# One excursion of ScalarE per block instead of two, and the first convolution on VectorE

## The reference

```
h1 = xg @ W1.T + b1 ; h2 = h1 @ W2.T + b2          # per group g of 512 tokens
xz = x @ Wi.T + bi                                   # 256 -> 1024
x_in, z = xz[..., :512], xz[..., 512:]
u  = silu(causal_depthwise_conv4(x_in) + conv_b)
dt = softplus(x_in[..., :32] @ Wdt.T + bdt)
A  = -exp(A_log)                                     # 512 x 16
h  = h * exp(dt_t * A) + dt_t * Bm * u_t             # per token, 512 x 16 states
y  = einsum('bdn,dn->bd', h, Cm)
out = (y * silu(z)) @ Wo.T + bo + x * mean(Dv)
```

## Time and profile before

| | us |
|---|---|
| median of 3 runs | 744.03 (739.25 to 746.37) |
| the profiled execution | 739.71 |
| its span, first to last instruction | 737.9 |
| VectorE busy | 648.1 |
| PE busy | 630.7 |
| ScalarE busy | 612.5 |
| GpSimd busy | 329.6 |

### The profile page before, as it was taken

One profiled execution on the slowest core, in us unless ns is written; L12 is line 12 of the kernel. 1 busy time (PEld: TensorE's weight loads), 2 busy tenths in 40 slices (PEclk: granted clock), 3 DMA queues, 4 the chain that ended last, 5 costly groups with the idle time before them and its releaser, 6 DMA issues.

```text
span 737.9 us, 8249 instructions
## 1 busy us (share of the span) xinstructions
PE 630.7 (85%) x2904; PEld 324.4 (44%) x2904; DVE 648.1 (88%) x443; ACT 612.5 (83%) x1077; POOL 329.6 (45%) x184
## 2 busy tenths in 40 slices
PE   7877986889886999999888999995894999698946
PEld 5632432264432365645344466542240473345524
DVE  2427855979999999999999999899999999999994
ACT  2487998689988998999798989999798888894771
POOL 0106202426799046897930638436992051080010
PEclk9997998899999899999898999999896999899979
DMA  8440747180738143160749170160608150705001
GB/s 286 169 171 16 233 138 228 58 256 9 280 116 298 69 151 105 38 235 24 275 144 301 42 256 2 52 234 29 228 15 271 50 207 24 261 15 214 30 0 58
DMA packets 40027, 103.08 MB, mean 140 GB/s; under 512 B 4081, under 2 KB 13041, under 8 KB 39985
## 3 DMA queue, kind: packets, MB, share of 16 engines
q1 hardware_dynamic: 37424, 94.40, 36.0%
q10 hardware_dynamic: 2560, 8.14, 4.9%
HBM read 23.08 MB, written 4.19 MB: 37 GB/s over the span
## 4 chain that ended last, share of the span: by engine, by line
PE 41%; ACT 33%; DVE 13%; DMA 6%; issue 5%; ACTq 1%; POOL 1%; SPq 0%; POOLq 0%; DVEq 0%
ACT G L1159 14%; DVE G L1328 11%; PE Y L1498 9%; PE MB L1526 6%; PE MB L1369 5%; PE MB L1443 4%; PE MB L1465 4%; ACT XN L976 3%; PE MB L1424 3%; ACT XI L1076 3%; PE MB L1476 2%; ACT L1129 2%; PE MB L1433 2%; DMA RV<-DW 2%; DMA W<-in_w 2%
## 5 line engine op out<-in xcount | busy, mean ns | idle before, releaser
L1328 DVE TENSOR_TENSOR_SCAN G<-G,RV 128x1024 f32<-128x1024 f32 (+3 forms) x256 | 535.7, 2153 | 33.9 <-ACT G L1159 19.3
L1159 ACT ACTIVATE G<-RD,COL 128x1024 f32<-128x1024 f32 (+1 forms) x288 | 279.5, 1043 | 19.2 <-PE Y L1498 16.7
L1498 PE MATMUL Y<-G,RW 128*32 128x512 f32 x1024 | 139.4, 660 | 39.5 <-DVE G L1328 39.5
L881 POOL TENSOR_SCALAR LV<-LV 128x4 f32<-128x4 f32 x18 | 19.7, 1097 | 227.2 <-ACT XN L976 227.0
L890 POOL TENSOR_TENSOR LV<-LV,HALF 128x4 f32<-128x4 f32 (+1 forms) x25 | 45.4, 1816 | 113.6 <-DVE LV L1222 112.1
L921 POOL TENSOR_SCALAR X<-X,LV 128x256 f32<-128x256 f32 x32 | 85.3, 2674 | 0.8
L1498 PEld LDWEIGHTS Y<-G,RW 128*32 128x32 f32 x1024 | 27.1, 114 | 117.0 <-DVE G L1328 61.0
L907 POOL TENSOR_SCALAR XN<-X,LV 128x256 f32<-128x256 f32 x36 | 76.8, 2137 | 1.9
L1465 PE MATMUL MB<-XI,DIAG 128*64 128x512 f32 x248 | 65.5, 666 | 13.9 <-DMA XI<-XI 13.9
L1526 PE MATMUL MB<-WO,ZS 128*128 128x256 f32 x256 | 62.7, 379 | 0.9 <-DVE ZS L1337 0.9
L1443 PE MATMUL MB<-XT,WI 128*128 128x512 f32 x128 | 62.5, 615 | 1.0 <-ACT XT L1002 1.0
(11 more groups left out here) (95 smaller groups left out, 777.1 us busy)
## 6 DMA issues: line engine op xcount, KB each, us to landing
RD<-DW SPq DMA_DIRECT2D x60, 512.0 KB, 3.8
RV<-DW SPq DMA_DIRECT2D x60, 512.0 KB, 5.3
W<-in_w SPq DMA_DIRECT2D x48, 256.5 KB, 4.0
XI<-XI ACTq DMA_DIRECT2D x30, 256.5 KB, 5.8
X<-in_x SPq DMA_DIRECT2D x8, 512.0 KB, 6.0
out<-X SPq DMA_DIRECT2D x7, 512.0 KB, 3.0
G<-in_w SPq DMA_DIRECT2D x4, 513.0 KB, 8.1
RV<-in_w SPq DMA_DIRECT2D x4, 513.0 KB, 12.9
```

The source lines that it names most:

```text
L1159: eng.activation(G[:, i % NG, 1 + t0:1 + t1], RD[:, q, t0:t1], ACT.Exp, scale=NAC[:, states(i):states(i) + 1]).then_inc(sems["exp"])
L1328: eng.tensor_tensor_scan(g[:, at:1 + t1], g[:, at:1 + t1], v[:, at:1 + t1], first, ALU.mult, ALU.add).then_inc(sems["scan"])
L1498: ins = eng.matmul(Y[32 * q:32 * q + 32, 512 * h:512 * h + 512], RW[:, states(i + o), :], G[:, (i + o) % NG, 512 * h + 1:512 * h + 513], s ...
```

## The change

It does nine things. (1) `dts` is dissolved: dm, the softplus load, dt, the silu load, u, the z of up to two blocks and the exp load stand in one stretch at the end of `proj`; "unset" is gone, so blocks 1 to 15 have three loads each and not four. (2) The convolution of the first half of block 0 is made by VectorE (`conv`: one multiplication by a tap, three multiply-adds over 512 tokens), out of an unsplit copy XC that ScalarE makes; the matrices DIAG0 and eight matmuls go. (3) Layernorms 0 to 3 and 23 take mean and variance by bn_stats and bn_aggr on VectorE, not by sums and squares. (4) All others centre with the mean: GpSimd's two instructions after 1/sqrt (L895, L900) become one before it (`mean`). (5) The shift DMAs of ten blocks (`SYNCED`) are issued by SP's queue. (6) VectorE takes over xi of block 1, the sums of layernorms 7 and 12, and the copies of layernorm 7's transposes. (7) The merge weights of the second group are loaded into ZS, not RV. (8) The order up to the first scans is given by a string, HEAD. (9) All tables of places are new.

```diff
-RATE, STORE = 220, 80
-FIRST = ["dts", "proj", "outs"]
+RATE, STORE = 300, 200
+FIRST = ["proj", "outs"]
...
-DTS, PROJ = (-21, -22, -25, -20), (-25, -25, -32, -27)
+PROJ = (-23, -26, -27, -26)
+MEET, LULL = 0, 3
...
-SENDS, LATE = (8, 9, 15, 15), (14, 14, 14, 15)
-REPD, REPL = 9, 11
+SENDS, LATE = (11, 11, 11, 15), (11, 12, 14, 12)
+REPD, REPL = 9, 9
...
+HEAD = "sscbcsccllbabllbalsbblsalbllllsl"
...
-VSUM, VXI, VXT = (), (), ()
+VSUM, VXI, VXT = (7, 12), ((1, 0), (1, 1)), (7,)
+SYNCED = (2, 3, 4, 6, 7, 8, 9, 10, 11, 12)
...
-    def dts(k):
...
-        yield from after(("w", k - 1, passes(k - 1) - 1))
-        yield 2
-        for hf in range(2):
-            do("dm", k, hf)
-        yield 0
-        do("softset", k, 0)
-        do("dt", k, 0)
-        do("unset", k, 0)
-
-    def proj(k):
...
+        if zs and zs[0] >= NZ:
+            yield from after(("opm", (zs[-1] - NZ) // 4, 1, 3))
+        for _ in range(MEET):
+            yield 0
+        yield from after(("repd", k - 1, 3, passes(k - 1) - 1), ("w", k - 1, passes(k - 1) - 1))
+        yield 2
+        for hf in range(2):
+            do("dm", k, hf)
         yield 0
+        do("softset", k, 0)
+        do("dt", k, 0)
         do("silu", k, 0)
         for hf in range(2):
             do("u", k, hf)
-        for ko in zs[:1]:
-            for hf in range(2):
-                do("z", ko, hf)
-        for ko in zs[1:]:
+        for ko in zs:
             for hf in range(2):
                 do("zm", ko, hf)
             for hf in range(2):
                 do("z", ko, hf)
         do("expset", k, 0)
-        yield from rest_for(REST)
-        yield from after(("dt", k, 0))
+        yield from rest_for(LULL)
         do("w", k, 0)
...
+                elif stage == "bn":
...
+                    for i in range(2):
-                        ins = eng.scalar_tensor_tensor(out=v[:, t, :], in0=bank("opa", *a)[:, 256 * i:256 * i + 256], scalar=1.0,
-                                                       in1=v[:, t, :], op0=ALU.mult, op1=ALU.add, accum_out=lv[:, 0, t:t + 1])
-                    ins.then_inc(sems["vop"])
+                        t = 2 * pr + i
+                        src = bank("fm", 0, 0, hf, pr)[:, 256 * i:256 * i + 256] if ph == 1 else v[:, t, :]
+                        ins = eng.bn_stats(out=gauge(c)[:, t, 0:6], in_=src)
+                    ins.then_inc(sems["bn"])
...
+                elif stage == "conv":
+                    e.wait_ge("xc", 0, 0)
+                    e.wait_ge("col")
+                    eng.tensor_scalar(CV, XC[:, 0:512], COL[:, CW0:CW0 + 1], None, ALU.mult).then_inc(sems["taps"])
+                    for t in range(1, 4):
+                        eng.wait_ge(sems["taps"], t)
+                        ins = eng.scalar_tensor_tensor(out=CV, in0=XC[:, t:t + 512], scalar=COL[:, CW0 + t:CW0 + t + 1], in1=CV,
+                                                       op0=ALU.mult, op1=ALU.add)
```

More of the change, by code:

```diff
@@ L114, in summed, with gauged @@
 def summed(c):
-    return "vsum" if early(c) or c in VSUM else "sum"
+    return "vsum" if c in VSUM else "sum"
+def gauged(c):
+    return c < 4 or c == 23
 def evac(k, hf):
-    return "vxi" if (k, hf) in VXI else "xi"
+    return "xc" if (k, hf) == (0, 0) else "vxi" if (k, hf) in VXI else "xi"
 def turned(c):
@@ L507, in begin @@
     def begin(k, s):
-        for first, chain in ((DTS, dts), (PROJ, proj)):
-            for ko in range(2, 16):
-                if 16 * k + s == 16 * ko + first[ko % 4]:
-                    yield chain(ko)
-        if (k, s) in PLAN["dts1"]:
-            yield dts(1)
+        for ko in range(2, 16):
+            if 16 * k + s == 16 * ko + PROJ[ko % 4]:
+                yield proj(ko)
         if (k, s) in PLAN["proj1"]:
@@ L541, in begin, with leads @@
             yield outs(3, 1)
+    def leads():
+        for i in range(LEAD):
+            do("exp", i)
+            yield 0
     def run(steps):
@@ L570, in schedule @@
     run(a)
+    do("diag")
     next(first)
     run(first)
-    for _ in range(3):
-        next(b)
+    do("rw")
     run(ffn(0, 0, 0))
-    for stage in ("diag", "rw"):
-        do(stage)
-    next(c)
-    for _ in range(5):
-        next(second)
-    next(c)
-    run(c)
-    a = half(0, 0)
-    for _ in range(4):
-        next(a)
-    next(second)
-    run(a)
-    run(b)
-    run(second)
-    next(late)
-    next(late)
-    for i in range(LEAD):
-        do("exp", i)
-    next(late)
-    next(late)
+    chains = {"a": half(0, 0), "b": b, "c": c, "s": second, "l": late, "e": leads()}
+    for name in HEAD:
+        next(chains[name], None)
+    for name in "cae":
+        run(chains[name])
+    for chain in (b, second):
+        needs[chain] = 0
     needs[late] = 0
@@ L956, in do @@
                     e.wait_ge(made("off", c), c)
-                    for i in range(4 if early(c) else 2):
+                    for i in range(4):
                         ins = eng.activation(xn[:, i, :], v[:, i, :], ACT.Identity, bias=lv[:, 4, i:i + 1],
@@ L1061, in do @@
                     if k:
-                        for hf in range(2):
+                        for hf in range(1 if k == 1 else 0, 2):
                             e.wait_ge("um", k - 1, hf)
@@ L1078, in do @@
                     ins.then_inc(sems["xi"])
-                elif stage == "sh":
+                elif stage == "sh" and a[0] not in SYNCED:
                     k, = a
-                    e.wait_ge("halo", k)
-                    e.wait_ge(evac(k, 1), k, 1)
+                    e.wait_ge(*(("halo", k) if k else ("xie",)))
+                    for hf in range(0 if k else 1, 2):
+                        e.wait_ge(evac(k, hf), k, hf)
                     c0 = 512 if k in HALVED else 0
@@ L1253, in do @@
                     if k:
-                        for h in range(2):
+                        for h in range(1 if k == 1 else 0, 2):
                             e.wait_ge("um", k - 1, h)
```

292 lines of the change are left out of this document (184 added, 108 removed), and 9 rows, old and new, of the table PLAN.

## The result

The changed kernel takes 777.82 us (median of four runs, 775.45 to 778.58) against 741.64 for the kernel before beside it: a ratio of 1.049, 95% interval 1.045 to 1.054. It is slower by 5%, where the prediction had 731. The profiled execution took 775.45 us, of which 773.7 are span. One run of experiment 12 (882.52 us at a granted clock of 0.72) and one of the kernel before beside it (1248.50) fell into a slow state and are left out of the times given there.

What follows compares the result with a forecast made beforehand. VectorE's scans were taken as the bound in blocks 2 to 15. Terms 0 - 1.9 - 5.6 - 2.4 + 0.5 = -9.4 on the profiled 739.7 gave 730.3, put down as 731, range 724 to 737.

Steps and rivals of the forecast that it cites:

- 41.3 forecast: Block 1: 38.8 us of VectorE work plus 2.5 waiting for the fourth RV; exp waits ahead of block 2 go; -5.6.
- up to the first scan: 0: Kernel start: no net gain, first scan at 46 to 49, second half of block 0 again near 81.0.
- the -1.9: End of block 0: block 1's first exp, and so its start, at 113.8 instead of 115.72.
- The end: Last layernorm half: gains the squares, loses by bn_aggr and bn_stats in VectorE's own row; +0.5 us.
- The step on SP's queue at the end of block 0: RV DMAs go right behind w, landing near 111; the queue's part of block 1's 9.32 us wait goes.
- Blocks 2 to 15: -2.4: Blocks 2 to 15: VectorE idle 8.7 us instead of 12.3, plus 1.2 for layernorm 12's sum; -2.4 us.
- The ones that it named: Waits in blocks 2 to 15: 3.4 us each for w of blocks 4 and 8, 1.9 at block 10.
- Costed at nothing except through VectorE's waits: Fifteen removed loads, 19.2 us of ScalarE, lie beside VectorE's scans with 65 us spare, so enter no sum.
- The slower one: Rival, chance 0.11: um waits for shift DMAs, so w is late, 2 us in each of ten blocks; 750.
- ScalarE is the bound: Rival, chance 0.13: ScalarE bounds through its chains; idle time of blocks 1 to 15 goes, -20.7, so 719.
- the three signs that the prediction named for being wrong: um waiting for shift DMAs in most blocks; bn_stats above 0.42 us; block 0's second half starting later than 84.
- Small terms: Start of kernel, on VectorE: bn_stats of 256 elements 0.33 us each, four convolution passes 0.6 to 0.7 each.

Runs made afterwards that it cites:

- experiment 12: experiment 5 with the latest place of w, and the RV DMA issue with it, after unit 12 of the block before instead of unit 11: 778.27 us, ratio 1.056.
- experiment 13: Kernel before, with four merge-weight loads on SP's queue moved behind all four RV DMAs of block 1: 733.73 us, ratio 0.993.
- experiment 5: Changed kernel with GpSimd's centring adding the negated mean instead of subtracting the mean, and the merge correction moved to VectorE: 744.88 us, ratio 1.006.
- experiment 1: Changed kernel with GpSimd's layernorm centring adding the negated mean (cheap form) instead of subtracting the mean (dear form): 758.18 us, ratio 1.022.
- correction on VectorE (3): Changed kernel, subtracting centring kept, with the merge-weight correction (L976) moved from GpSimd to VectorE: 758.67 us, ratio 1.025.
- experiment 9: experiment 5 with the exp table loaded once more between dt and silu in each of 15 excursions: 758.76 us, ratio 1.026.
- experiment 11: Changed kernel with additive centring, but two excursions per block, 67 loads, the old tables and no shift DMA on SP's queue: 742.76 us, ratio 1.002.
- experiment 4: Kernel before with 15 GpSimd instructions of three forms added at its end, alone and then beside 40 scans; run once for its profile, no kernel time given.
- experiment 8: Changed kernel with GpSimd's residual scalings (L970) made over 4 of their 256 columns: 770.83 us, ratio 1.042.

## Why the prediction was wrong

**What held, and what met by luck.** Block 1 took 41.7 us (41.3 forecast, before 46.9), and 41.4 to 42.8 in the eight kernels with one excursion in the new order. This step is right in size, with a wait of 3.02 us for an RV (2.5 taken), though for the third RV and not the fourth. The moments before it look as good, first scan at 45.71 (46 to 49), second half of block 0 at 80.51 (81.0), block 1 at 114.17 (113.8) and released by an exp, but they meet by luck. In the ten kernels with the new order up to the first scan it comes anywhere from 45.7 to 49.4, and here it came 2.6 us before that of the kernel before. Counted from the first scan, the second half came after 34.8 us and not 32.7 (34.7 to 35.7 in these ten, 32.6 to 33.3 in the four with the old start): a loss of 2 us that "up to the first scan: 0" had at nothing. From there to block 1 it took 33.7 and not 34.7 (31.5 to 33.7 in the eight): the -1.9 is there, if small in this execution.

```profile
45.71 3.45 DVE L1425 TENSOR_TENSOR_SCAN G<-G,RV 128x512 f32<-128x512 f32 x3 [2.43 <-DMA RV<-DW]
114.17 4.47 DVE L1425 TENSOR_TENSOR_SCAN G<-G,RV 128x1024 f32<-128x1024 f32 x2 [2.33 <-ACT G L1228]
121.67 4.50 DVE L1425 TENSOR_TENSOR_SCAN G<-G,RV 128x1024 f32<-128x1024 f32 x2 [3.02 <-DMA RV<-DW]
```

The end took 18.2 us from the end of the last scan (755.51), before 17.8 (720.08): +0.4 (+0.5 taken). The step on SP's queue at the end of block 0 is shown by itself in experiment 13.

**The step that failed is "Blocks 2 to 15: -2.4".** It came out at +42.2 (599.6 us from block 2's first scan to the end of the last, before 557.4), with 55.7 us of VectorE idle where the step had 8.7. It priced w behind ScalarE's excursion and asked nothing of GpSimd, whose two parts in the change, the form of L956 and the order of its list, had no term anywhere in the sum: 32.1 of the 44.6 us between -2.4 and +42.2 go when both are undone (experiment 5, 567.5 us). The other 12.5 are the step's own waits, sized too small: in experiment 5 VectorE is idle for 21.6 us there, waits for u come to 10.2 us (6.8 taken) and waits for exps to 7.7 (1.9). The ones that it named are at about their prices: w of blocks 4 and 8 wait 2.58 and 4.29 us (3.4 taken, 2.2 to 4.9 as bounds), block 10's exps 2.35 (1.9). It missed w of block 6 (2.36) and of block 14 (0.95), and exps of block 6, 4.07 us behind an excursion with the gates of two blocks. That one takes 12.0 us (load at 335.13, first exp at 347.24), where the prediction had 10, since z waits between its halves for its projection on TensorE.

**How GpSimd's work reaches VectorE.** Experiments 1, 3 and 5 show that 33 of the 36 us hang on it. The traces show where. Lengths in us, from a block's first scan to the next one's (block 15: to its last scan's end):

| block | before | changed | cheap form (1) | correction on VectorE (3) | both (5) |
|---|---|---|---|---|---|
| 3 | 39.1 | 52.5 | 46.4 | 40.7 | 41.2 |
| 7 | 39.0 | 51.2 | 52.5 | 45.4 | 42.5 |
| 6 | 41.3 | 45.9 | 45.9 | 46.4 | 46.4 |
| 11 | 38.6 | 42.8 | 38.1 | 43.0 | 38.1 |
| 12 | 37.8 | 40.9 | 37.2 | 40.8 | 37.2 |
| 15 | 39.7 | 44.3 | 39.7 | 44.3 | 39.7 |
| the other eight | 321.9 | 321.9 | 321.4 | 323.3 | 322.4 |

Net, the whole loss lies in six blocks. Blocks 3 and 7 hold TensorE's two longest waits for a correction (9.41 and 7.23 us), and moving the correction mends most of them; blocks 11, 12 and 15 are mended by the cheap form alone; block 6 has the long excursion, and neither touches it. That the two fixes work for the most part at different places is why they nearly add up.

For block 7 the path stands above. Block 3 lost as much, by waits for exps and MS, and its path begins in the same way: four scalings, the correction, TensorE's transposes. Behind these stands the red, behind the red the exps:

```profile
189.80 16.12 POOL L970 TENSOR_SCALAR X<-X,LV 128x256 f32<-128x256 f32 x4
211.95 1.12 PE L1476 MATMUL MB<-COL,MS 128*128 128x128 f32 x4 [9.41 <-POOL MS L976]
218.94 1.92 PE L1585 MATMUL Y<-G,RW 128*32 128x512 f32 x16
220.93 4.27 ACT L1228 ACTIVATE G<-RD,COL 128x1024 f32<-128x1024 f32 x4 [2.79 <-PE Y L1585]
222.11 2.29 DVE L1425 TENSOR_TENSOR_SCAN G<-G,RV 128x1024 f32<-128x1024 f32 x1 [5.88 <-ACT G L1228]
228.70 0.16 DVE L1270 SCALAR_TENSOR_TENSOR MV<-MS,MSS 128x2 f32<-128x2 f32 x1 [4.29 <-ACT MS L1060]
```

In block 11 it begins with a centring in the dear form (L956, 7.18 us, from 545.53), which TensorE's transposes of a layernorm await:

```profile
552.77 1.97 PE L1496 MATMUL MB<-COL,XN 128*128 128x128 f32 x8 [6.03 <-POOL XN L956]
557.24 4.27 ACT L1228 ACTIVATE G<-RD,COL 128x1024 f32<-128x1024 f32 x4 [6.49 <-PE Y L1585]
572.04 6.66 DVE L1425 TENSOR_TENSOR_SCAN G<-G,RV 128x1024 f32<-128x1024 f32 x3 [3.25 <-ACT G L1228]
```

With the cheap form (experiment 1) VectorE waits for nothing in block 11. For blocks 12 and 15 the path was not followed.

**The loads.** "Costed at nothing except through VectorE's waits" was right in kind, and the waits were too few: eleven w with less slack than a load, not three waits (experiment 9). Yet a kernel with the load saved and GpSimd's share undone (745) is no faster than one with two excursions (743, experiment 11). These two differ in all tables and in the correction, so they do not price the excursion. What it is worth with places made for it, and whether tables exist in which it gains, was not tried and stays open.

**The rivals.** The slower one had the right sign and the right place (w late, then block k + 1) and another cause: no um of the changed kernel waits over 3.4 us for a shift DMA (before, 6.5); in experiment 12 one waits 9.2. Its 0.11 was too little, since it stood for one cause of late w when there were several: whatever delays um does. "ScalarE is the bound" is out: also in experiment 5, with GpSimd's share undone, ScalarE is 37.5 us lighter than before and the time is no shorter. None of the three signs that the prediction named for being wrong came up in force (bn_stats took 0.423 us on average out of PSUM, against 0.42): they asked nothing of GpSimd either.

**Small terms.** A bn_stats took 0.415 us from SBUF and 0.423 out of PSUM (0.33 taken, 0.42 the upper bound), and the aggregation 0.155. The four steps of the convolution took 0.49 and three times 0.75 (0.6 to 0.7 taken).

## What to carry to other kernels

Price every engine that a diff touches, also one that is busy for only 45%: what counts is whether another engine's list has an instruction that waits for it, and what stands behind that. Beside back-to-back scans a GpSimd instruction lasts as long as it waits, whatever its size, so take instructions off its list or put what others wait for ahead. Where places are set by a table, a small change shifts everything behind it: an isolated move of four DMAs gave 0.7%, a change of one table cost over 4%. Measure a stretch from an event that the change does not touch: here the first scan's time alone moves by 3 us.

## What the runs showed of the hardware

- GpSimd's tensor_scalar on 128x256 float32, with no scan beside it: 0.546 to 0.556 us as (mult, add) or (add, mult), 1.21 to 1.22 as (subtract, mult) (experiment 4). On 4 columns (mult, add) took 0.34 at the least (experiment 8).
- Beside back-to-back scans of 1024: 4.55 us, two scans, in each of the three forms (experiment 4); with 4 columns in the kernel still 2.08 on average, with 256 columns 2.23 (experiment 8).
- Every second scan beside them starts 0.15 us later than it would (2.34 us after the one before and not 2.18 to 2.20, experiment 4).
- A table load is followed by its first activation within 0.02 us, also where two loads stand back to back (experiment 9: 400.25 and 401.54, u at 402.84).
